# Half of the unmasked row maxima of a causal attention taken from key differences

## What is computed

```python
x = x + 0.5 * ffn(layernorm(x))
# attention on layernorm(x): q (2, 32, 1024, 8), k and v (2, 8, 1024, 8), rotary positions on q and k
scores = einsum('bhqd,bhkd->bhqk', q, k_rep) / sqrt(8)
scores = where(kpos > qpos, -inf, scores)
attn = softmax(scores)              # subtracts the row maximum
x = x + (attn @ v_rep) @ Wo + bo
x = x + 0.5 * ffn(layernorm(x))
```

## Time and profile before

| what | value |
|---|---|
| three executions | 801.71, 802.96, 804.95 us |
| span of the profiled execution | 799.2 us |
| mean granted TensorE clock | 0.974 |
| busy: TensorE, VectorE, ScalarE, GpSimd | 752.0, 712.8, 487.9, 263.3 us |
| one steady group of the attention | 24.12 us |

### The profile page before, as it was taken

One profiled execution on the slowest core, in us unless ns is written; L12 is line 12 of the kernel. 1 busy time (PEld: TensorE's weight loads), 2 busy tenths in 40 slices (PEclk: granted clock), 3 DMA queues, 4 the chain that ended last, 5 costly groups with the idle time before them and its releaser, 6 DMA issues.

```text
span 799.2 us, 15470 instructions
## 1 busy us (share of the span) xinstructions
PE 752.0 (94%) x5168; PEld 503.9 (63%) x5168; DVE 712.8 (89%) x1857; ACT 487.9 (61%) x949; POOL 263.3 (33%) x359
## 2 busy tenths in 40 slices
PE   4899999988999999999999999999999999999996
PEld 3677887886855444554444544444544577888886
DVE  4989999988598999999999999999996459989997
ACT  6454443321124888888888888888888634344451
POOL 1143535027742222333222332255335211533330
PEclk9999999999965999999999999999999999999998
DMA  8100000015753033431133321633223000000001
GB/s 305 44 12 1 1 1 1 1 52 185 218 179 68 11 70 76 89 73 43 40 76 75 75 62 47 159 78 76 62 55 75 16 8 1 1 27 1 27 1 52
DMA packets 23551, 48.83 MB, mean 61 GB/s; under 512 B 3784, under 2 KB 10568, under 8 KB 22960
## 3 DMA queue, kind: packets, MB, share of 16 engines
q1 hardware_dynamic: 23408, 47.78, 22.8%
q10 hardware_dynamic: 64, 0.07, 0.0%
HBM read 19.83 MB, written 14.35 MB: 43 GB/s over the span
## 4 chain that ended last, share of the span: by engine, by line
PE 64%; DVE 19%; POOL 6%; issue 5%; ACT 4%; DMA 1%; PEldq 0%; PEld 0%; SPq 0%; DVEq 0%; ACTq 0%; POOLq 0%
PE att_o_ps L1422 18%; PE att_s_ps L1406 15%; PE att_m_ps L1371 11%; PE ffn_gate L218 6%; PE ffn_up L218 5%; PE ffn_y_ps L351 5%; DVE ffn_hs L524 3%; DVE ffn_h L566 3%; POOL qkv_turned L859 2%; POOL qkv_parts L864 2%; PE att_m_ps L1379 1%; DVE att_scratch L1471 1%; DVE ffn_rank L510 1%; DVE ffn_pair_max L498 1%; PE out_y_ps L1162 1%
## 5 line engine op out<-in xcount | busy, mean ns | idle before, releaser
L1524 ACT ACTIVATE att_probs<-att_s_ps 128x512 f32<-128x512 f32 x630 | 305.7, 555 | 54.7 <-PE att_s_ps L1406 52.9
L1471 DVE CUSTOM_DVE_ANT_0 att_scratch<-att_m_ps,att_causal 128x512 bf16<-128x512 f32 (+3 forms) x512 | 221.1, 486 | 7.7 <-PE att_m_ps L1371 6.1
L1371 PE MATMUL att_m_ps<-k,q 64*128 64x512 f32 (+3 forms) x768 | 222.8, 399 | 2.4 <-DVE att_maxima L1471 1.9
L1406 PE MATMUL att_s_ps<-q,k 64*128 64x512 f32 (+2 forms) x756 | 209.9, 384 | 2.7 <-ACT att_probs L1524 1.0
L1406 PEld LDWEIGHTS att_s_ps<-q,k 64*128 64x128 f32 x756 | 118.2, 188 | 97.0 <-ACT att_probs L1524 91.5
L1474 DVE TENSOR_REDUCE att_maxima<-att_m_ps 128x1 f32<-128x512 f32 x256 | 161.9, 684 | 7.2 <-PE att_m_ps L1371 7.1
L1422 PE MATMUL att_o_ps<-att_probs,att_vs 128*32 128x512 f32 (+3 forms) x1536 | 158.5, 500 | 3.2 <-POOL att_probs L1563 1.6
L1563 POOL TENSOR_SCALAR_AFFINE_SELECT att_probs<-att_probs 128x512 f32<-128x512 f32 x128 | 80.0, 637 | 245.3 <-ACT att_probs L1524 245.3
L1371 PEld LDWEIGHTS att_m_ps<-k,q 64*128 64x128 f32 x768 | 128.1, 193 | 42.0 <-DVE att_maxima L1471 24.4
L630 POOL TENSOR_TENSOR ffn_hs_lo<-ffn_hs,ffn_hs_hi 128x512 fp32r<-128x512 f32 x48 | 76.7, 1622 | 106.5 <-ACT ffn_hs_hi L427 106.5
L454 ACT ACTIVATE ffn_a<-ffn_h 128x512 f32<-128x512 f32 x64 | 40.5, 633 | 106.3 <-DVE ffn_h L566 106.3
(11 more groups left out here) (117 smaller groups left out, 1176.5 us busy)
## 6 DMA issues: line engine op xcount, KB each, us to landing
q_rows<-qkv_parts SPq DMA_DIRECT2D x16, 512.0 KB, 4.0
q<-q_rows SPq DMA_DIRECT2D x16, 512.0 KB, 4.7
q<-q SPq DMA_DIRECT2D x16, 512.0 KB, 4.3
q<-att_shift_t SPq DMA_DIRECT2D x132, 4.0 KB
k_rows<-qkv_parts SPq DMA_DIRECT2D x8, 256.0 KB, 3.0
k<-k_rows SPq DMA_DIRECT2D x16, 128.0 KB, 4.9
k<-k SPq DMA_DIRECT2D x16, 128.0 KB, 4.6
out_num<-att_sums SPq DMA_DIRECT2D x128, 16.0 KB
```

The source lines that it names most:

```text
L1371: pe.matmul(m_ps[unit_bank(n)][:, COLUMNS[m]], q[g % 2][m_lane, h, t * P:(t + 1) * P], k[g % 2][m_lane, kc * N:kc * N + cols], start=True, ...
L1406: last = pe.matmul(s_all[S_BANK[n]][:, at:at + w], k[g % 2][lane, kb * P:(kb + 1) * P], q[g % 2][lane, h, qc * N + q0:qc * N + q0 + w], st ...
L1471: dve.tensor_tensor_reduce(out=scratch[bank][:, at], in0=m_ps[bank][:, at], in1=causal[:, N - n:], scale=1.0, scalar=LOWEST, op0=ALU.add, ...
L1524: act.activation(probs[u % len(probs)][:, h, SPAN[u]], s_all[S_BANK[n]][:, SPAN[u]], ACT.Exp, scale=SCALE).then_inc(exp_done, 1)
```

## The change

Of the 16 unmasked maxima units of a group, every other one (8, the `G` above) is made in another way. Let a be the first 256 keys of the chunk and b the second 256. The row maximum of all 512 scores is the maximum of b + max(a-b, 0). During the projections GpSimd makes the differences of the keys' first and second half of the first chunk of each batch, and they are stored beside the keys as 256 further columns. TensorE fills the bank with two matmuls of 256 columns, one of the differences and one of b. ScalarE writes max(a-b, 0) to one of three buffers in SBUF (`take_gain`), and VectorE takes the row maximum of b plus that in one instruction of 256 columns. ScalarE's gains stand in its order where the `m` step stands in `ORDER`. `ORDER`, the 4 banks and the 3 score banks stay as they are. The k tiles grow from 1024 to 1280 columns. One scratch buffer and the new buffers move to another region of memory. `has_differences` holds for unit 2 (the keys) of chunks 0 and 2. The core of the diff:

```diff
@@ qkv_programs, gpsimd
+            ready = keys_ready if has_differences(c, u) else turned_ready
+            pool.tensor_tensor(turned[:, u, :], by_cos[:, u, :], by_sin[:, u, :], ALU.add).then_inc(ready, 1)
+            if has_differences(c, u):
+                pool.wait_ge(keys_ready, c // 2 + 1)
+                first, second = turned[KV:, u, :DIFFERENCES], turned[KV:, u, DIFFERENCES:2 * DIFFERENCES]
+                pool.tensor_tensor(first, first, second, ALU.subtract).then_inc(turned_ready, 1)
@@ qkv_programs, sync: store(c)
+                    if has_differences(c, u):
+                        src = parts[KV:, u, part, :DIFFERENCES].bitcast(F32)
+                        sp.dma_start(k_rows[:, part::PARTS, key_columns(c)[1]],
+                                     src[:, None, :].to_broadcast([KV, PARTS, DIFFERENCES])).then_inc(stored[u][part], 16)
@@ GroupRows
+            self.k.append(region.take(f"k{e}", [P, self.K_COLUMNS], F32R))
@@ maximum_scores
+        if m in PAIRED:
+            pe.matmul(ps[:, :HALF], queries, keys[:, T:T + HALF], start=True, stop=True)
+            pe.matmul(ps[:, HALF:], queries, keys[:, HALF:N], start=True, stop=True).then_inc(m_done, 1)
@@ m_unit (VectorE)
+        if m in PAIRED:
+            i = pairs_by(g * MU + m) - 1
+            wait_apart(dve, gain_ready, i + 1, passed)
+            dve.tensor_tensor_reduce(out=scratch[bank][:, :HALF], in0=m_ps[bank][:, HALF:], in1=gains[i % GAINS][:], scale=1.0,
+                                     scalar=LOWEST, op0=ALU.add, op1=ALU.max, accum_out=top_of).then_inc(m_taken, 1)
+            return
@@ scalar
+        def take_gain(n):
+            i = pairs_by(n) - 1
+            act.wait_ge(m_done, n + 1)
+            if i >= GAINS:
+                act.wait_ge(m_taken, paired_unit(i - GAINS) + 1)
+            act.activation(gains[i % GAINS][:], m_ps[unit_bank(n)][:, :HALF], ACT.Relu).then_inc(gain_ready, 1)
@@ scalar, lead-in: the same order as TensorE's, gains included
+        for kind, n in lead_in():
+            if kind == "s":
+                exponentials(n)
+            elif kind == "t":
+                take_shift(n)
+            elif n % MU in PAIRED:
+                take_gain(n)
@@ scalar, group
+                elif kind == "m" and n % MU in PAIRED:
+                    take_gain(n)
```

More of the change, by code:

```diff
@@ L707, in qkv_programs, with has_differences, key_columns @@
     fills = hooks["fills"]
+    DIFFERENCES = group_rows.DIFFERENCES
+    assert 2 * N == T and 2 * KV == P and 2 * DIFFERENCES == N
+    def has_differences(c, u):
+        return u == QM and c % 2 == 0
+    def key_columns(c):
+        start = c * N // T * group_rows.K_COLUMNS
+        return bass.ds(start + c * N % T, N), bass.ds(start + T, DIFFERENCES)
     def first_scores(pe):
@@ L968, in copy_s @@
         sp.wait_ge(self.m_loaded[e], 16 * self.LOADS * (g // 2 + 1))
-        for tile in (self.q[e], self.k[e]):
+        for tile in (self.q[e][:], self.k[e][:, :self.T]):
             sp.dma_start(tile[self.s_rows].bitcast(F32), tile[self.m_rows].bitcast(F32)).then_inc(self.s_loaded[e], 16)
@@ L1017, in __init__ @@
         self.den_cols = [(rows.stop - rows.start) * N // P for rows in self.ROW_SPANS]
-        self.den_parts = [hole.take(f"out_den_parts{b}", [P, cols], F32) for b, cols in enumerate(self.den_cols)]
+        self.den_parts = [hole.take(f"out_den_parts{b}", [P, cols], F32, over=at + 4 * sum(self.den_cols[:b]))
+                          for b, cols in enumerate(self.den_cols)]
+        assert at + 4 * sum(self.den_cols) <= hole.at
         self.y_ps = y_banks
@@ L1235, in attention_programs, with pairs_by, paired_unit @@
     assert len(M_UNITS) == MU and all(sum(unit[3] for unit in fill) == N for fill in M_FILLS)
+    PAIRED = [m for i, m in enumerate(m for m, (t, _, kc, _) in enumerate(M_UNITS) if kc < t // TPC) if i % 2]
+    PU = len(PAIRED)
+    HALF = group_rows.DIFFERENCES
+    GAINS = 3
+    assert all(COLUMNS[m] == slice(0, N) and M_UNITS[m][2] == 0 for m in PAIRED) and 2 * HALF == N
+    def pairs_by(n):
+        return n // MU * PU + sum(m <= n % MU for m in PAIRED)
+    def paired_unit(i):
+        return i // PU * MU + PAIRED[i % PU]
     AHEAD = 2
@@ L1273, in steps, with lead_in @@
                 yield kind, n
+    def lead_in():
+        heads = 0
+        for kind, n in first_steps:
+            yield kind, n
+            if kind == "m" and (n >= MU or (n >= S_FROM and (n - S_FROM) % 2 == 0)) and heads < FIRST_HEADS:
+                yield "s", heads
+                heads += 1
     first_steps = [*(("m", n) for n in range(FIRST_TURNS[0])), ("t", 0), *(("m", n) for n in range(FIRST_TURNS[0], MU + FIRST_TURNS[1])),
@@ L1290, in sb, with in_hole @@
         return region.take(f"att_{name}", shape, dt)
+    def in_hole(name, shape, dt):
+        return output.hole.take(f"att_{name}", shape, dt)
     def sem(name):
@@ L1297, in attention_programs @@
     causal = sb("causal", [P, N], F32)
-    scratch = [sb(f"scratch{i}", [P, N], BF16) for i in range(M_BANKS)]
+    scratch = [(sb if i else in_hole)(f"scratch{i}", [P, N], BF16) for i in range(M_BANKS)]
+    gains = [in_hole(f"gains{i}", [P, HALF], F32) for i in range(GAINS)]
     maxima = sb("maxima", [P, QPK, KB, QC], F32)
@@ L1537, in take_sums @@
             act.activation(sums[qc][:], o_ps[:], ACT.Copy).then_inc(o_taken, 1)
-        take_shift(0)
-        for n in range(FIRST_HEADS):
-            exponentials(n)
-        take_shift(1)
+        for kind, n in lead_in():
+            if kind == "s":
[4 more added lines that the diff above has]
+                take_gain(n)
         ended = []
```

47 lines of the change are left out of this document (25 added, 22 removed).

## The result

| what | before | after |
|---|---|---|
| median of 4 executions on one chip (range) | 802.44 us (801.71 to 804.95) | 838.47 us (836.85 to 839.57) |
| ratio, 95% interval | | 1.0453 [1.0433, 1.0473] |
| span of the profiled execution | 799.2 us | 837.2 us |
| mean granted TensorE clock | 0.974 | 0.969 |

The changed kernel is 4.5% slower, 36.0 us where 16.6 were forecast. That is outside the range given (796 to 832 us): the sign was right, the size was not. The 38.0 us of span fall, by the starts of the copies of the sums (one series of them to a group), in four places: up to the first copy +3.4 us; the 15 passes that carry maxima +32.6, or 2.17 each; the last pass +1.1; everything after it +1.0 (kernels that differ only in the attention scatter by as much there). So one steady group tells the story: the one from 335.04 to 361.25 us is 26.21 us long, where 24.12 was before.

What follows compares the result with a forecast made beforehand. TensorE, VectorE and ScalarE were nearly full and tied by the written order. 1.1+0.2+0.2-0.35 = 1.15 us a group over 14 passes gave +16.1, plus 0.5 for projections and lead-in: +16.6, 819.6 us median, range 796 to 832.

Steps and rivals of the forecast that it cites:

- the third item of the walk: Gains queued behind ScalarE's exponentials make VectorE and TensorE's fills wait: 0.2 us a group, bounds 0 and 0.6.
- ScalarE late in stretches 1 to 4: Six gains, 1.7 us, on ScalarE less waits of 0.55: 1.1 us a group late, passed to TensorE.
- in 5 and 6: One gain each on ScalarE delays the third exponential; about 0.1 us each passes on: 0.2 us, bounds 0 and 0.56.
- Relief in stretches 7 to 10: VectorE arrives with less backlog, so TensorE's waits for it shrink: gain of 0.35 us a group, bounds 0 and 0.65.
- Projections and lead-in: GpSimd's subtractions, ScalarE's later end and the first gain's wait, less VectorE's relief: +0.5 us, bounds -1 and +1.5.
- The prices of single instructions: VectorE's 256-column maxima 0.35 us, ScalarE's gains 0.28 (at most 0.49), GpSimd's subtraction 0.4 to 0.73.
- bare weight load: Rival on TensorE: the second 256-column matmul waits for its weight load, 21 us on top, 841 us; chance 0.03.
- The lock of banks and gains: Rival: walk's second and third items reach their upper bounds, 1.9 us a group, 830 us; chance 0.22.
- The faster rival: VectorE was the bound and ScalarE fits the gains; relief of 0.65 us a group at most, 792 us; chance 0.17.
- The forecast's last sentence: Sign in the steady group: if it is over 25.8 us, the waits for maxima banks should carry the excess.
- TensorE's waits for exponentials: Sign at the score heads: waits longer than 5.9 us a group if right; not longer if wrong.
- Table loads: Rival on ScalarE: loads between gains and exponentials cost hundreds of us; chance 0.02 for the change not doing what it says.

Runs made afterwards that it cites:

- load and relief: Changed kernel, but ScalarE's gains come from a constant and VectorE's 256-column maxima use a constant, so nobody waits for gains: 1.0146 of the kernel before.
- the one unit: Changed kernel with one split unit a group, the first of stretch 4, its gain behind three exponentials and the copy of the sums: 1.0322 of the kernel before.
- the load alone: Changed kernel with 512-wide units again; ScalarE makes its 8 gains a group from an SBUF tile and nobody waits for them: 1.0172 of the kernel before.
- Relief alone: Changed kernel without gains on ScalarE; split banks stay and VectorE's 256-column maxima take a constant as second operand: 0.9992 of the kernel before.
- the projections alone: Changed kernel with no unit split: key differences are made, stored and loaded, attention as before: 1.0019 of the kernel before.
- one unit and its drain eased: One split unit behind the sums, plus the unmasked unit two fills later made 256 wide with a constant and no gain: 1.0299 of the kernel before.

## Why the prediction was right in sign and wrong in size

- **The step that failed is the third item of the walk**, the gains queued behind exponentials: "Not shown by any row; bounds 0 and 0.6 us [...]; I take **0.2 us**." It measured 1.4 us a group (load and relief against the change), over twice its upper bound, 24.6 us in all. The place was named rightly: stretch 4's gain, about 2 us behind its matmul. What was wrong is the sentence after it, "VectorE ran up to 2 us behind TensorE before too, so part of this is hidden". VectorE being behind is no cover for a later VectorE, because the banks it has not emptied are the ones that TensorE needs next. The bound was taken by the length of an instruction; it had to be worked out as wait plus drain. From the rows of before that was to be had (timelines of ScalarE and of TensorE before the change):

```profile
334.01 1.58 ACT L1524 ACTIVATE att_probs<-att_s_ps 128x512 f32<-128x512 f32 x3
...
336.19 1.07 PE L1422 MATMUL att_o_ps<-att_probs,att_vs 128*32 128x512 f32 x8
```

  The gain comes behind the second of these three exponentials, at 334.01+2 x 0.49 = 334.99, and ends 0.38 us later, at 335.37 (the narrow exponential). With 0.18 us until VectorE starts and the drain of 0.35+0.69+0.69+0.05+0.44, the value unit starts at 337.77 instead of 336.19: 1.6 us, which is what the one unit cost. The 0.18, the 0.05 and the 0.44 are from the later traces; without them it is 0.9, still above the bound.
- **ScalarE late in stretches 1 to 4 (1.1 us) and in 5 and 6 (0.2)** was over-sized: together 0.74 us measured by the load alone. The steps' split was off too: 0.38 in stretches 2 and 3, nothing in 4, and 0.37 in 5 and 6. In the load alone ScalarE did work without a listed pause through these stretches, but it carried part of its lateness past stretch 6 to where it has time to spare (a pause of 0.19 us there, 0.32 before), which the forecast ruled out with "the lateness passes to TensorE".
- **Relief in stretches 7 to 10 (0.35 us)** was zero. Relief alone leaves all four within 0.01 us. What it brings lies in stretch 3, 0.18 us, and with the load beside it there is nothing left of that. The waits of 0.26 us at the transposes are not for VectorE's backlog, as they stand with 1.5 us more of spare time on it.
- **Projections and lead-in** were +0.5 forecast and +3.4 measured. VectorE's wait for the first gain was as forecast (1.9; 1.81 in the row below), and the projections alone brought 1.0 us. The 2.0 us of relief set against it were not there: the lead-in with relief alone ended only 0.4 us before that with the projections alone. The forecast also counted one wait, and the trace has six: between 222 and 264 us VectorE waits 5.8 us for gains. Counted from GpSimd's first instruction of the projections, the first copy of the sums comes after 86.5 us before, 87.8 with the projections alone and also with load and relief, and 90.0 in the change. The 2.2 us over the projections alone, at the same mean clock, go with these waits. The rest can't be apportioned, because the granted clock differs as well. Over 222 to 264 us its mean is 0.59 before and 0.55 in the change and with the projections alone, mostly at the lower of its two levels, 1.2 GHz; from 200 to 224 us it was 1.00 before and in the change, with TensorE busy 5.8 and 6.0 of the last 7 us. The kernel with one unit and its drain eased had 0.67 and ended the lead-in at 258.7 us, the one without the eased unit 0.55 and 263.0.

Timeline of VectorE in the changed kernel, the first gain:

```profile
229.97 0.42 DVE L1532 CUSTOM_DVE_ANT_0 att_scratch<-att_m_ps,att_gains 128x256 bf16<-128x256 f32 x1 [1.81 <-ACT att_gains L1600]
```

- **The prices of single instructions held.** VectorE's new form takes 343.09-342.74 = 0.35 us, a gain 0.26 to 0.28 us from its start to the next exponential's, and GpSimd's subtraction was at its upper bound. The split costs TensorE no bare weight load.
- **The rivals.** The lock of banks and gains was the right mechanism, but its 830 us took the same 0.6 us bound. The faster rival is refuted by the relief alone, and the reading it stood on, "VectorE is busy 97% of the group", did not mean that easing VectorE helps: 2.0 us less work brought 0.18 us a group. The forecast's last sentence (over 25.8 us, the waits for maxima banks carry the excess) came true, and VectorE's new waits for gains are there as said. Two signs were wrong. TensorE's waits for exponentials went down (5.3 us), which the forecast had named as a sign of being wrong; I read it as TensorE arriving late at them, which no run shows by itself. And stretches 1 and 6 did not grow, while stretch 7 grew by 0.09 us.
- **Table loads.** No load stands between gains and exponentials in the changed kernel's timeline; the attention has one, as before. That agrees with what the Trainium skill says of relu ("ScalarE: Activation LUTs", on table sets). The same page's advice to put relu on VectorE was not tested here. What the runs show is that the function was cheap on ScalarE (0.26 us) and its place in ScalarE's order was not.

## What to carry to other kernels

Before moving work to an engine with idle time, look at what stands ahead of it in that engine's order at the moment when its result is needed; the total of idle time says nothing of that. Price a late operand for an in-order consumer of a ring of buffers as the wait plus the emptying of every filled slot that the producer's next milestone needs, less what the stretch took before. Where several engines are nearly full and tied by one order, as here, easing one can bring next to nothing (0.18 us of 2.0) while delaying it costs nearly in full (1.6 us for a wait of 1.76), so try the relief by itself first: if that brings nothing, no way of paying for it can. Not tried here: a ring of more than four maxima banks, which might give a late gain more room.

## What the runs showed of the hardware

**Two weight loads in one row group hide.** The timeline of TensorE in the changed kernel, a split unit and the next, and of its weight loads:

```profile
348.66 0.27 PE L1434 MATMUL att_m_ps<-k,q 64*128 64x256 f32 x1
348.77 0.28 PE L1435 MATMUL att_m_ps<-k,q 64*128 64x256 f32 x1
...
348.89 0.39 PE L1437 MATMUL att_m_ps<-k,q 64*128 64x512 f32 x1
...
348.66 0.18 PEld L1435 LDWEIGHTS att_m_ps<-k,q 64*128 64x128 f32 x1
...
348.77 0.18 PEld L1437 LDWEIGHTS att_m_ps<-k,q 64*128 64x128 f32 x1
```

The matmuls start 0.11 and 0.12 us apart, though each has a weight load of its own that lasts 0.18 us, and the loads run while the matmul before them in the same rows is running. Of the 112 split units of 14 steady passes 27 have their two matmuls so close, most others 0.22 us apart. The rule of the Trainium skill ("TensorE: Matmul & The Clock Gate", on what overlaps), that a load overlaps a running matmul only in another row group, doesn't hold for these. The same page also lets a load go ahead when it targets a background weight buffer; these rows fit that, but can't tell where the load went.

**GpSimd's time doesn't fall with the partitions.** Its 64x256 subtraction takes 0.72 us, as long as the 128x256 addition, 0.73 us. Timeline of GpSimd in the changed kernel:

```profile
184.15 0.72 POOL L877 TENSOR_TENSOR qkv_turned<-qkv_turned 64x256 f32<-64x256 f32 x1
```

**From the end of a gain on ScalarE to VectorE's start pass 0.18 us.** The gain that ended at 344.92 let VectorE start at 345.10, and the change's other gains that VectorE waited for did the same. A bank goes back faster: the one that VectorE finished at 345.52 was filled from 345.59, 0.07 us later. It comes free at the end of VectorE's instruction, 0.42 us after its start, and not at the 0.35 us after which VectorE starts the next.
